# A latent attention and routed FFN layer: the 128-wide plain float32 products made into three products of high and low parts

## The chip, the cores and the metric

The kernel runs on one core of one Trainium2 chip. The metric is the device time of one execution in microseconds, the median of three runs.

## What is computed

A post-norm layer on `x[2, 512, 256]`: attention whose keys and values are one shared latent per position, then an FFN on the half of the positions that a router picks.

```python
k = x @ W_lat + b_lat                                  # [2, 512, 128], keys and values of all heads
q = (x @ W_d + b_d).reshape(Bx, Tx, NH, L)             # 16 heads of 128
att = jnp.einsum('bhtl,bsl->bhts', q, k) * scale
att = softmax(where(causal, att, -inf))
y = jnp.einsum('bhts,bsl->bhtl', att, k)
x = layernorm(x + (y @ W_proj + b_proj))
scores = jnp.einsum('bsd,d->bs', x, router_weight) + router_bias[0]
top_scores, indices = top_k(scores, 256)
processed = gelu(x[indices] @ w1 + b1) @ w2 + b2
x = layernorm(x.at[indices].add(processed * sigmoid(top_scores)))
```

## The kernel before

A unit is one head of one batch entry; there are 32. The 512 positions are four tiles of 128. Each engine has its own program of periods, and period p works on several units at once: scores of unit p, turning and values of unit p - 1, output projection of unit p - 2, queries of unit p + 1. The engines meet at semaphores alone, and each keeps its program order.

Nearly every product is done in three parts. Both operands are kept as a high part (rounded to float32r) and a low part (the remainder), and `product` (lines 359 to 364) issues high x high (L362), high x low (L363) and low x high (L364) into one PSUM bank. In the trace each of these is one weight load and one matmul. Two products are plain float32 instead, each one call in the code and two weight loads with two matmuls in the trace:

- line 441, in `scores`: the scores of the first query tile (j = 0), 128 queries against 128 keys, from `qT_first` and `kT`;
- line 511, in `values`: the last key tile's part of the values (i = 3), from `k_last` and `pT_last`, into the last 128 columns of `ps_y`.

Their operands are made on ScalarE (ACT): line 685 writes `qT_first` from the queries' PSUM bank, and line 687 the high part of the other 384 columns; VectorE (DVE) then writes their low part at line 836. For the probabilities, which TensorE (PE) turns by transposes (line 461, three groups in `turn`, listed in `turns` at line 225), the third group holds i = 3 and i = 2: line 723 copies i = 3 as `pT_last`, line 724 takes the high part of i = 2 and line 889 (DVE) its low part. For the keys themselves, once for each batch entry, line 703 writes `k_last`, line 704 and line 858 the parts of the other three tiles.

PE's order within a period, in the middle of the loop, is: scores of j = 3 and 2; turns 0 and 1; scores of j = 1 and 0; queries of the next unit (six matmuls of 512 columns); turn 2; projection (twelve matmuls of 256 columns); values i = 0 to 3. The matmuls that need `qT_lo` are the first scores of the next period; those that need the third turn's parts are the values of i = 2 and 3. After period 17 DVE adds the projection of the first batch entry to `x1` (`take_out`, line 1005, half by half), and the first projection of the second entry waits for it in period 18.

Of the kernel before, what the change touches and what calls it, by code (L numbers as in the profile page):

```python
# [28 lines left out]
F32 = mybir.dt.float32  # L29
F32R = mybir.dt.float32r  # L30
BF16 = mybir.dt.bfloat16
ACT = mybir.ActivationFunctionType
ALU = mybir.AluOpType

P = 128
BATCH, SEQ, DIM = 2, 512, 256
HEADS, LAT = 16, 128
FFN = 1024
KEEP = SEQ // 2
TILES = SEQ // P  # L40
# [9 lines left out]
P_OFF = [P * (j * (j + 1) // 2) for j in range(TILES)]  # L50
P_COLS = P * TILES * (TILES + 1) // 2

PT_OFF = {2: 0, 1: 2 * P, 0: 5 * P}
PT_COLS = 9 * P


def mk_layer_kernel(nc, x, W_lat, b_lat, W_d, b_d, W_proj, b_proj, router_w, router_b,
                    w1, b1, w2, b2, out):
    with ExitStack() as top:
        def sb(name, shape, dt=F32, stack=top):  # L60
            return stack.enter_context(nc.sbuf_tensor(name, shape, dt))

        def sem(name):
            return top.enter_context(nc.semaphore(name))
# [19 lines left out]
        bias_cols = sb("bias_cols", [P, BIASES])  # L84
# [37 lines left out]
        ps_s3, ps_s2, ps_s10, ps_t0, ps_t1, ps_y = bank  # L122
        ps_q = ps_s3
# [3 lines left out]
        def sems(name):  # L127
# [10 lines left out]
        x_turned, x_hi_done, x_split, x1_started = sem("x_turned"), sem("x_hi_done"), sem("x_split"), sem("x1_started")  # L138
        kT_ready, kT_done, kT_hi_done, kT_split = (
            sem(n) for n in ("kT_ready", "kT_done", "kT_hi_done", "kT_split"))  # L140
        k_turned, k_last_done, k_hi_done, k_split = (
            sem(n) for n in ("k_turned", "k_last_done", "k_hi_done", "k_split"))
        wd_hi_done, wd_split = sem("wd_hi_done"), sem("wd_split")
        wp_hi_done, wp_split = sem("wp_hi_done"), sem("wp_split")
        wf_hi_done, wf_split = sem("wf_hi_done"), sem("wf_split")
        q_ready, q_first_done, q_hi_done, q_lo_done = (
            sem(n) for n in ("q_ready", "q_first_done", "q_hi_done", "q_lo_done"))
        mask_done = sem("mask_done")
        scores_ready, negmax_done, exp_done, rinv_done = (
            sem(n) for n in ("scores_ready", "negmax_done", "exp_done", "rinv_done"))  # L150
        norm_act, norm_dve = sem("norm_act"), sem("norm_dve")
        pt_ready, pt_last_done, pt_hi_done, pt_lo_done = (
            sem(n) for n in ("pt_ready", "pt_last_done", "pt_hi_done", "pt_lo_done"))
        y_ready, y_hi_done, y_lo_done = sem("y_ready"), sem("y_hi_done"), sem("y_lo_done")
        proj_done, proj_half, out_taken = sem("proj_done"), sem("proj_half"), sem("out_taken")
        stats_done, aggr_done, var_done, rstd_done, ln_done = (
# [17 lines left out]
        def wait(eng, s, value):  # L174

            if not isinstance(value, int) or value > 0:
                eng.wait_ge(s, value)


        att = ExitStack()  # L180
# [5 lines left out]
        kT = [sb(f"kT{b}", [P, SEQ], F32, att) for b in range(BATCH)]  # L186
        kT_hi = [sb(f"kT_hi{b}", [P, SEQ], F32R, att) for b in range(BATCH)]
        kT_lo = [sb(f"kT_lo{b}", [P, SEQ], F32R, att) for b in range(BATCH)]
        k_hi = [sb(f"k_hi{b}", [P, TILES - 1, LAT], F32R, att) for b in range(BATCH)]
        k_lo = [sb(f"k_lo{b}", [P, TILES - 1, LAT], F32R, att) for b in range(BATCH)]  # L190
        k_last = [sb(f"k_last{b}", [P, LAT], F32, att) for b in range(BATCH)]

        wd_raw = [sb(f"wd_raw{s}", [P, CH, LAT], F32, att) for s in range(2)]
        wd_hi = [sb(f"wd_hi{s}", [P, CH, LAT], F32R, att) for s in range(2)]
# [2 lines left out]
        wp_hi = [sb(f"wp_hi{s}", [P, DIM], F32R, att) for s in range(2)]  # L197
        wp_lo = [sb(f"wp_lo{s}", [P, DIM], F32R, att) for s in range(2)]

        qT_first = [sb(f"qT_first{s}", [P, P], F32, att) for s in range(2)]  # L200
        qT_hi = [sb(f"qT_hi{s}", [P, SEQ], F32R, att) for s in range(2)]
        qT_lo = [sb(f"qT_lo{s}", [P, SEQ], F32R, att) for s in range(2)]
        yT_hi, yT_lo = sb("yT_hi", [P, SEQ], F32R, att), sb("yT_lo", [P, SEQ], F32R, att)
        probs = [sb(f"probs{s}", [P, P_COLS], F32, att) for s in range(2)]
        pT_last = sb("pT_last", [P, P], F32, att)
        pT_hi, pT_lo = sb("pT_hi", [P, PT_COLS], F32R, att), sb("pT_lo", [P, PT_COLS], F32R, att)
        att.close()

# [9 lines left out]
        def p_tile(s, j):  # L218
# [5 lines left out]

        turns = [([0], ps_t0, ps_t0[:, :], slice(PT_OFF[0], PT_OFF[0] + 4 * P)),
                 ([1], ps_t1, ps_t1[:, 0:3 * P], slice(PT_OFF[1], PT_OFF[1] + 3 * P)),
                 ([3, 2], ps_t0, ps_t0[:, P:3 * P], slice(PT_OFF[2], PT_OFF[2] + 2 * P))]

        class Period:

# [71 lines left out]
        ps_k = ps_out[:, 2:4, :].rearrange("p a d -> p (a d)")  # L302
# [55 lines left out]
        def _(pe):  # L358
            def product(dst, left, right, first=True, last=True, check=False):

                (lh, ll), (rh, rl) = left, right
                pe.matmul(dst, lh, rh, start=first, stop=False, skip_group_check=check)  # L362
                pe.matmul(dst, lh, rl, start=False, stop=False, skip_group_check=check)  # L363
                return pe.matmul(dst, ll, rh, start=False, stop=last, skip_group_check=check)  # L364
# [51 lines left out]
            for c in range(CH):  # L416
                last = product(ps_q[:, :], (wd_hi[0][:, c, :], wd_lo[0][:, c, :]),
                               (xT_hi[0][:, c, :], xT_lo[0][:, c, :]), c == 0, c == CH - 1)
# [5 lines left out]
            def scores(at, js):  # L424
                p, b, s = at.p, at.batch(0), at.place(0)
                if at.fixed == b * HEADS:
                    pe.wait_ge(kT_split, b + 1)
                    pe.wait_ge(kT_done, b + 1)
                for j in js:
                    n = (j + 1) * P  # L430
                    dst = score_bank[j]
                    if j == 3:
                        wait(pe, q_lo_done, p + 1)
                    if j:
                        wait(pe, negmax_done, p * 4 - {3: 3, 2: 2, 1: 0}[j])
                    t = slice(j * P, (j + 1) * P)
                    if j:
                        last = product(dst, (qT_hi[s][:, t], qT_lo[s][:, t]), (kT_hi[b][:, 0:n], kT_lo[b][:, 0:n]))
                    else:
                        wait(pe, q_first_done, p + 1)  # L440
                        last = pe.matmul(dst, qT_first[s][:, :], kT[b][:, 0:P], start=True, stop=True)  # L441
                    if j != 1:
                        last.then_inc(scores_ready, 1)

# [52 lines left out]
            def values(at):  # L497

                p, b = at.p, at.batch(-1)
                if at.fixed - 1 == b * HEADS:  # L500
                    pe.wait_ge(k_split, b + 1)
                    pe.wait_ge(k_last_done, b + 1)
                wait(pe, y_lo_done, p - 1)
                for i in range(TILES - 1):
                    wait(pe, pt_lo_done, p * 3 - 2 + i)
                    n = (TILES - i) * P
                    t = slice(PT_OFF[i], PT_OFF[i] + n)
                    product(ps_y[:, SEQ - n:], (k_hi[b][:, i, :], k_lo[b][:, i, :]),
                            (pT_hi[:, t], pT_lo[:, t]), i == 0, False)
                wait(pe, pt_last_done, p)  # L510
                pe.matmul(ps_y[:, SEQ - P:], k_last[b][:, :], pT_last[:, :], start=False, stop=True).then_inc(y_ready, 1)  # L511


            def turn_scores(b, dst):
# [164 lines left out]
        def _(act):  # L679
            def split_queries(k, place, head):  # L680

                wait(act, q_ready, k + 1)
                wait(act, scores_ready, k * 3 - 3)
                bias = bias_cols[:, bass.ds(head, 1)]
                act.activation(qT_first[place][:, :], ps_q[:, 0:P], ACT.Identity, bias=bias,
                               scale=1.0).then_inc(q_first_done, 1)
                act.activation(qT_hi[place][:, P:], ps_q[:, P:], ACT.Identity, bias=bias,  # L687
                               scale=1.0).then_inc(q_hi_done, 1)

            def x_high(b):  # L690
# [9 lines left out]

            def k_high(b):
                act.wait_ge(k_turned, b + 1)
                act.copy(k_last[b][:, :], ps_k[:, SEQ - P:]).then_inc(k_last_done, 1)
                act.copy(k_hi[b][:, :, :], ps_k[:, 0:SEQ - P].rearrange("p (j l) -> p j l", l=LAT)).then_inc(k_hi_done, 1)

            x_high(0)
            act.wait_ge(bias_done, 1)
# [11 lines left out]

            def turned(at, n):  # L720
                wait(act, pt_ready, at.p * 3 - 2 + n)
                if n == 2:
                    act.copy(pT_last[:, :], ps_t0[:, 0:P]).then_inc(pt_last_done, 1)
                act.copy(pT_hi[:, turns[n][3]], turns[n][2]).then_inc(pt_hi_done, 1)  # L724

            def period(at):
# [100 lines left out]
            for j in range(TILES):  # L827
                act.wait_ge(minus_mean_done, j // 2 + 1)
                act.activation(squared[:, j, :], x1[:, TILES + j, :], ACT.Square, bias=minus_mean[:, j:j + 1],  # L829
                               scale=1.0, accum_out=squares[:, j:j + 1]).then_inc(squares_done, 1)  # L830

        @block.vector
        def _(dve):
            def queries_low(k, place, head):
                wait(dve, q_hi_done, k + 1)
                dve.scalar_tensor_tensor(qT_lo[place][:, P:], ps_q[:, P:], bias_cols[:, bass.ds(head, 1)],  # L836
                                         qT_hi[place][:, P:].bitcast(F32), ALU.add, ALU.subtract).then_inc(q_lo_done, 1)

            dve.memset(still[:, :], 0.0).then_inc(still_filled, 1)

# [14 lines left out]

            def k_low(b):
                dve.wait_ge(k_hi_done, b + 1)
                dve.tensor_tensor(k_lo[b][:, :, :], ps_k[:, 0:SEQ - P].rearrange("p (j l) -> p j l", l=LAT),
                                  k_hi[b][:, :, :].bitcast(F32), ALU.subtract).then_inc(k_split, 1)

            dve.wait_ge(wlat_in, 16)
# [308 lines left out]
            for half in range(2):  # L1170
                for j in range(2 * half, 2 * half + 2):
                    add_up(1, j)
                t = slice(2 * half, 2 * half + 2)
# [3 lines left out]
            for half in range(2):  # L1177
                t = slice(2 * half, 2 * half + 2)
# [146 lines left out]
```

## Time and profile before

| | us |
|---|---|
| median of 3 runs | 300.29 (300.2 to 300.47) |
| the profiled execution | 299.99 |
| its span, first to last instruction | 298.3 |
| PE busy (matmuls) | 287.2 (96% of the span) |
| PEld busy (weight loads, beside PE) | 261.6 (88%) |
| DVE busy | 223.0 (75%) |
| ACT busy | 211.8 (71%) |
| POOL busy | 143.3 (48%) |

The granted clock of PE is full in 39 of the 40 slices of the page. A matmul's record is longer than the time by which it holds up the next one, since matmuls are pipelined, so their cost is read from start to start. The same holds, to a lesser degree, for ACT and DVE, whose records overlap a little.

### The profile page before, as it was taken

To read this page: it belongs to the slowest core of one execution; us is meant where nothing else is said; L and a number is where in the kernel's file an instruction comes from. 1 tells how busy PE (TensorE), PEld (TensorE's weight loads), DVE (VectorE), ACT (ScalarE), POOL (GpSimd) and SP (SyncE) were. 2 spreads that over 40 slices of the span, in tenths; PEclk is the share of its full clock that TensorE was granted. 3 is DMA by queue.
4 is the path that set the end of the run, shared out by engine and by line. 5 is a ranking of instruction groups with operands and counts; after the bars stand their busy time and mean duration, and the time that the engine had idled before them with its cause. 6 is when DMAs were issued, how large, how long until landed. Compare 5 with 4: busy or idle time off the path is not lost.

```text
span 298.3 us, 6300 instructions
## 1 busy us (share of the span) xinstructions
PE 287.2 (96%) x1942; PEld 261.6 (88%) x1942; DVE 223.0 (75%) x698; ACT 211.8 (71%) x582; POOL 143.3 (48%) x201
## 2 busy tenths in 40 slices
PE   7999999999999999999989999999999999999990
PEld 4787999999999999999889999999999999999990
DVE  3688777777777777777878788989778877497674
ACT  3588777777777777777767777777788777663622
POOL 3557533333333358555554755556556512183011
PEclk9999999999999999999999999999999999999998
DMA  6582111111111111111110111111110000000012
GB/s 196 105 302 72 52 37 35 35 35 35 34 33 30 39 41 34 35 32 36 32 36 18 34 37 35 38 35 35 38 36 20 19 21 0 2 1 0 2 45 96
DMA packets 17738, 13.42 MB, mean 45 GB/s; under 512 B 1433, under 2 KB 17458, under 8 KB 17714
## 3 DMA queue, kind: packets, MB, share of 16 engines
q1 hardware_dynamic: 17714, 13.13, 15.0%
q8 instruction: 12, 0.20, 0.2%
q14 instruction: 12, 0.10, 0.1%
HBM read 12.07 MB, written 1.05 MB: 44 GB/s over the span
## 4 chain that ended last, share of the span: by engine, by line
PE 87%; DVE 6%; ACT 2%; issue 1%; SPq 1%; DMA 1%; POOLq 0%; DVEq 0%; ACTq 0%
PE bank L362 17%; PE bank L364 16%; PE bank L363 16%; PE bank L461 11%; PE ps_out L362 6%; PE ps_out L364 6%; PE ps_out L363 6%; PE bank L511 2%; PE bank L441 2%; DVE x L1043 1%; DMA bias_rows<-in_L_ffn_b 1%; DVE x L1005 1%; ACT squared L829 1%; DVE sel L1051 1%; PE bank L550 1%
## 5 line engine op out<-in xcount | busy, mean ns | idle before, releaser
L717 ACT ACTIVATE probs<-probs,negmax 128x512 f32<-128x512 f32 (+3 forms) x128 | 72.6, 574 | 6.9 <-DVE negmax L882 5.5
L1197 POOL TENSOR_TENSOR wd_hi<-wd_raw,zero 128x256 fp32r<-128x256 f32 x32 | 24.6, 769 | 95.7 <-DVE probs L937 89.6
L724 ACT CAST pT_hi<-bank 128x512 fp32r<-128x512 f32 (+2 forms) x96 | 43.5, 488 | 33.1 <-PE bank L461 33.1
L889 DVE TENSOR_TENSOR pT_lo<-bank,pT_hi 128x512 fp32r<-128x512 f32 (+2 forms) x96 | 53.0, 553 | 11.1 <-ACT pT_hi L724 11.1
L882 DVE CUSTOM_DVE_ANT_0 probs<-bank,mask_row 128x512 f32<-128x512 f32 (+3 forms) x128 | 59.1, 482 | 0.6 <-PE bank L364 0.6
L461 PE MATMUL bank<-ident,probs 128*128 128x128 f32 x320 | 45.3, 272 | 0.0
L461 PEld LDWEIGHTS bank<-ident,probs 128*128 128x128 f32 x320 | 38.5, 140 | 5.3 <-issue 0.2
L362 PE MATMUL ps_out<-wp_hi,yT_hi 128*128 128x256 f32 x128 | 38.5, 301 | 1.1 <-DVE x L1005 1.1
L362 PE MATMUL bank<-kT_hi,qT_hi 128*128 128x512 f32 (+2 forms) x96 | 37.7, 393 | 0.2 <-DVE qT_lo L836 0.2
L899 DVE TENSOR_TENSOR yT_lo<-bank,yT_hi 128x512 fp32r<-128x512 f32 x32 | 22.1, 691 | 21.0 <-PE bank L364 14.8
L364 PE MATMUL ps_out<-wp_hi,yT_lo 128*128 128x256 f32 x128 | 36.2, 283 | 0.0
L363 PE MATMUL ps_out<-wp_lo,yT_hi 128*128 128x256 f32 x128 | 36.1, 282 | 0.0
L362 PE MATMUL bank<-pT_hi,k_hi 128*128 128x512 f32 (+2 forms) x96 | 32.9, 343 | 0.6 <-DVE pT_lo L889 0.6
L364 PE MATMUL bank<-kT_hi,qT_lo 128*128 128x512 f32 (+2 forms) x96 | 32.7, 340 | 0.0
L363 PE MATMUL bank<-pT_lo,k_hi 128*128 128x512 f32 (+2 forms) x96 | 32.4, 337 | 0.0
L363 PE MATMUL bank<-kT_lo,qT_hi 128*128 128x512 f32 (+2 forms) x96 | 32.3, 337 | 0.0
L364 PE MATMUL bank<-pT_hi,k_lo 128*128 128x512 f32 (+2 forms) x96 | 32.2, 335 | 0.0
L1197 POOL TENSOR_TENSOR wp_hi<-wp_raw,zero 128x256 fp32r<-128x256 f32 x32 | 23.6, 737 | 14.2 <-DVE probs L937 14.2
L756 ACT ACTIVATE probs<-probs,rinv 128x512 f32<-128x512 f32 x32 | 23.2, 726 | 8.2 <-DVE rinv L931 8.2
L937 DVE TENSOR_SCALAR probs<-probs,rinv 128x384 f32<-128x384 f32 (+2 forms) x96 | 28.1, 350 | 1.1
L836 DVE SCALAR_TENSOR_TENSOR qT_lo<-bank,bias_cols,qT_hi 128x384 fp32r<-128x384 f32 x32 | 19.8, 617 | 11.9 <-ACT qT_hi L687 11.4
L362 PE MATMUL bank<-xT_hi,wd_hi 128*128 128x512 f32 x64 | 27.9, 435 | 0.0
(148 smaller groups left out, 742.0 us busy)
## 6 DMA issues: line engine op xcount, KB each, us to landing
wd_raw<-in_L_attn_W_d SPq DMA_DIRECT2D x32, 128.0 KB, 2.2
wp_raw<-in_L_attn_W_proj SPq DMA_DIRECT2D x32, 128.0 KB, 2.1
wf_raw<-in_L_ffn_w SPq DMA_DIRECT2D x2, 1024.0 KB, 7.1
x_nat<-in_L_attn_x SPq DMA_DIRECT2D x4, 256.0 KB, 2.9
out<-x SPq DMA_DIRECT2D x3, 256.0 KB, 2.2
out<-x SPq DMA_DIRECT2D x2, 128.0 KB, 1.9
wlat_raw<-in_L_attn_W_lat SPq DMA_DIRECT2D x1, 128.0 KB, 3.3
bproj_all<-in_L_attn_b_proj SPq DMA_DIRECT2D x1, 128.0 KB, 3.5
```

Source lines behind the costliest of these rows:

```text
L362: pe.matmul(dst, lh, rh, start=first, stop=False, skip_group_check=check)
L363: pe.matmul(dst, lh, rl, start=False, stop=False, skip_group_check=check)
L364: return pe.matmul(dst, ll, rh, start=False, stop=last, skip_group_check=check)
L461: last = pe.transpose(dst[:, a:a + P], p_tile(s, j)[:, i * P:(i + 1) * P], ident[:, :])
L717: act.activation(p_tile(s, j), p_tile(s, j), ACT.Exp, bias=negmax[:, s, j:j + 1], scale=-1.0, accum_out=sums[:, s, j:j + 1]).then_inc(exp_ ...
L724: act.copy(pT_hi[:, turns[n][3]], turns[n][2]).then_inc(pt_hi_done, 1)
L756: act.mul(p_tile(at.place(0), 3), p_tile(at.place(0), 3), rinv[:, at.place(0), 3:4]).then_inc(norm_act, 1)
L882: dve.tensor_tensor_reduce(p_tile(s, j), score_bank[j], mask_row[:, (TILES - 1 - j) * P:], -SCALE, -MASKED, ALU.add, ALU.min, accum_out=ne ...
L889: dve.tensor_tensor(pT_lo[:, dst], src, pT_hi[:, dst].bitcast(F32), ALU.subtract).then_inc(pt_lo_done, 1)
L899: dve.tensor_tensor(yT_lo[:, :], ps_y[:, :], yT_hi[:, :].bitcast(F32), ALU.subtract).then_inc(y_lo_done, 1)
L937: dve.tensor_scalar(p_tile(s, j), p_tile(s, j), rinv[:, s, j:j + 1], None, ALU.mult).then_inc(norm_dve, 1)
L1197: pool.tensor_tensor(hi, src, nothing, ALU.add).then_inc(hi_done, 1)
```

## The change

The two plain products become calls of `product`. With them `qT_first`, `k_last` and `pT_last`, their semaphores and the ACT instructions that wrote them go; the instructions that write the high and low parts of queries, keys and of the third turn grow by 128 columns. The number of matmuls of these two products goes from 2 to 3 each, and all six become float32r matmuls with 128 moving columns.

```diff
-PT_OFF = {2: 0, 1: 2 * P, 0: 5 * P}
-PT_COLS = 9 * P
+PT_OFF = {3: 0, 2: P, 1: 3 * P, 0: 6 * P}
+PT_COLS = 10 * P
...
-                 ([3, 2], ps_t0, ps_t0[:, P:3 * P], slice(PT_OFF[2], PT_OFF[2] + 2 * P))]
+                 ([3, 2], ps_t0, ps_t0[:, 0:3 * P], slice(PT_OFF[3], PT_OFF[3] + 3 * P))]
...
-                    if j:
-                        last = product(dst, (qT_hi[s][:, t], qT_lo[s][:, t]), (kT_hi[b][:, 0:n], kT_lo[b][:, 0:n]))
-                    else:
-                        wait(pe, q_first_done, p + 1)
-                        last = pe.matmul(dst, qT_first[s][:, :], kT[b][:, 0:P], start=True, stop=True)
+                    last = product(dst, (qT_hi[s][:, t], qT_lo[s][:, t]), (kT_hi[b][:, 0:n], kT_lo[b][:, 0:n]))
...
-                for i in range(TILES - 1):
-                    wait(pe, pt_lo_done, p * 3 - 2 + i)
+                for i in range(TILES):
+                    if i < TILES - 1:
+                        wait(pe, pt_lo_done, p * 3 - 2 + i)
                     n = (TILES - i) * P
                     t = slice(PT_OFF[i], PT_OFF[i] + n)
-                    product(ps_y[:, SEQ - n:], (k_hi[b][:, i, :], k_lo[b][:, i, :]),
-                            (pT_hi[:, t], pT_lo[:, t]), i == 0, False)
-                wait(pe, pt_last_done, p)
-                pe.matmul(ps_y[:, SEQ - P:], k_last[b][:, :], pT_last[:, :], start=False, stop=True).then_inc(y_ready, 1)
+                    last = product(ps_y[:, SEQ - n:], (k_hi[b][:, i, :], k_lo[b][:, i, :]),
+                                   (pT_hi[:, t], pT_lo[:, t]), i == 0, i == TILES - 1)
+                last.then_inc(y_ready, 1)
...
-                act.activation(qT_first[place][:, :], ps_q[:, 0:P], ACT.Identity, bias=bias,
-                               scale=1.0).then_inc(q_first_done, 1)
-                act.activation(qT_hi[place][:, P:], ps_q[:, P:], ACT.Identity, bias=bias,
+                act.activation(qT_hi[place][:, :], ps_q[:, :], ACT.Identity, bias=bias,
                                scale=1.0).then_inc(q_hi_done, 1)
...
-                act.copy(k_last[b][:, :], ps_k[:, SEQ - P:]).then_inc(k_last_done, 1)
-                act.copy(k_hi[b][:, :, :], ps_k[:, 0:SEQ - P].rearrange("p (j l) -> p j l", l=LAT)).then_inc(k_hi_done, 1)
+                act.copy(k_hi[b][:, :, :], ps_k.rearrange("p (j l) -> p j l", l=LAT)).then_inc(k_hi_done, 1)
...
-                if n == 2:
-                    act.copy(pT_last[:, :], ps_t0[:, 0:P]).then_inc(pt_last_done, 1)
                 act.copy(pT_hi[:, turns[n][3]], turns[n][2]).then_inc(pt_hi_done, 1)
...
-                dve.scalar_tensor_tensor(qT_lo[place][:, P:], ps_q[:, P:], bias_cols[:, bass.ds(head, 1)],
-                                         qT_hi[place][:, P:].bitcast(F32), ALU.add, ALU.subtract).then_inc(q_lo_done, 1)
+                dve.scalar_tensor_tensor(qT_lo[place][:, :], ps_q[:, :], bias_cols[:, bass.ds(head, 1)],
+                                         qT_hi[place][:, :].bitcast(F32), ALU.add, ALU.subtract).then_inc(q_lo_done, 1)
...
-                dve.tensor_tensor(k_lo[b][:, :, :], ps_k[:, 0:SEQ - P].rearrange("p (j l) -> p j l", l=LAT),
+                dve.tensor_tensor(k_lo[b][:, :, :], ps_k.rearrange("p (j l) -> p j l", l=LAT),
                                   k_hi[b][:, :, :].bitcast(F32), ALU.subtract).then_inc(k_split, 1)
```

## Rows read from the trace of the kernel before

**Rows 1.** The page: part 1 (busy us) and part 4 (chain that ended last)

```profile
PE 287.2 (96%) x1942; PEld 261.6 (88%) x1942; DVE 223.0 (75%) x698; ACT 211.8 (71%) x582; POOL 143.3 (48%) x201
...
PE 87%; DVE 6%; ACT 2%; issue 1%; SPq 1%; DMA 1%; POOLq 0%; DVEq 0%; ACTq 0%
```

**Rows 2.** Waits of PE: us in total, times, longest us

```profile
PE ps_out L362 <- DVE x L1005: 1.1, 1, 1.1
PE bank L362 <- DVE pT_lo L889: 0.6, 1, 0.6
```

**Rows 3.** Timeline, PE, one period: start us, us, engine, line, out<-in

```profile
121.70 0.28 PE L364 MATMUL bank<-pT_hi,k_lo 128*128 128x256 f32 x1
121.81 0.39 PE L511 MATMUL bank<-pT_last,k_last 128*128 128x128 f32 x2
121.95 0.47 PE L362 MATMUL bank<-kT_hi,qT_hi 128*128 128x512 f32 x1
122.27 0.39 PE L363 MATMUL bank<-kT_lo,qT_hi 128*128 128x512 f32 x1
122.50 0.40 PE L364 MATMUL bank<-kT_hi,qT_lo 128*128 128x512 f32 x1
...
124.39 0.38 PE L441 MATMUL bank<-kT,qT_first 128*128 128x128 f32 x2
...
124.84 0.40 PE L363 MATMUL bank<-xT_lo,wd_hi 128*128 128x512 f32 x1
...
128.99 0.28 PE L362 MATMUL bank<-pT_hi,k_hi 128*128 128x256 f32 x1
```

**Rows 4.** Timeline, PEld (weight loads), the same period, around L441

```profile
124.27 0.31 PEld L441 LDWEIGHTS bank<-kT,qT_first 128*128 128x128 f32 x2
124.50 0.19 PEld L362 LDWEIGHTS bank<-xT_hi,wd_hi 128*128 128x128 f32 x1
124.61 0.19 PEld L363 LDWEIGHTS bank<-xT_lo,wd_hi 128*128 128x128 f32 x1
```

**Rows 5.** Timeline, PEld, the first two loads after a stall

```profile
23.48 0.19 PEld L362 LDWEIGHTS bank<-pT_hi,k_hi 128*128 128x128 f32 x1 [0.97 <-DVE pT_lo L889]
23.59 0.19 PEld L363 LDWEIGHTS bank<-pT_lo,k_hi 128*128 128x128 f32 x1
```

**Rows 6.** Bf16 loads: timeline of ten matmuls, then line 525 (ns min/median/max)

```profile
214.07 0.39 PE L525 MATMUL bank<-ones_bf,beats 128*128 128x1 bf16 x10
...
L525 PEld LDWEIGHTS bank<-ones_bf,beats x20: 95/96/100, 214.0 to 271.8; 128*128 128x128 bf16 x20
```

**Rows 7.** Groups by shape, ACT: busy us, mean ns, idle before

```profile
L687 ACT ACTIVATE qT_hi<-bank,bias_cols 128x384 fp32r<-128x384 f32 x32 | 18.2, 570 | 0.0
...
L724 ACT CAST pT_hi<-bank 128x384 fp32r<-128x384 f32 x32 | 15.6, 486 | 0.0
...
L724 ACT CAST pT_hi<-bank 128x256 fp32r<-128x256 f32 x32 | 12.5, 390 | 0.0
L685 ACT ACTIVATE qT_first<-bank,bias_cols 128x128 f32<-128x128 f32 x32 | 11.3, 354 | 1.0 <-PE bank L364 1.0
L723 ACT COPY pT_last<-bank 128x128 f32<-128x128 f32 x32 | 8.4, 262 | 0.0
...
L698 ACT ACTIVATE kT_hi<-ps_out,bias_cols 128x512 fp32r<-128x512 f32 x2 | 1.4, 678 | 2.1 <-PE ps_out L364 2.1
```

**Rows 8.** Groups by shape, DVE

```profile
L836 DVE SCALAR_TENSOR_TENSOR qT_lo<-bank,bias_cols,qT_hi 128x384 fp32r<-128x384 f32 x32 | 19.8, 617 | 11.9 <-ACT qT_hi L687 11.4
L889 DVE TENSOR_TENSOR pT_lo<-bank,pT_hi 128x384 fp32r<-128x384 f32 x32 | 17.7, 552 | 0.0
...
L889 DVE TENSOR_TENSOR pT_lo<-bank,pT_hi 128x256 fp32r<-128x256 f32 x32 | 13.3, 415 | 0.3 <-ACT pT_hi L724 0.3
...
L853 DVE SCALAR_TENSOR_TENSOR kT_lo<-ps_out,bias_cols,kT_hi 128x512 fp32r<-128x512 f32 x2 | 1.5, 737 | 2.0 <-ACT kT_hi L698 2.0
```

**Rows 9.** Timeline, DVE, the third turn's low part in the same period

```profile
127.84 0.41 DVE L889 TENSOR_TENSOR pT_lo<-bank,pT_hi 128x256 fp32r<-128x256 f32 x1
```

More of the change, by code:

```diff
@@ L140, in mk_layer_kernel @@
             sem(n) for n in ("kT_ready", "kT_done", "kT_hi_done", "kT_split"))
-        k_turned, k_last_done, k_hi_done, k_split = (
-            sem(n) for n in ("k_turned", "k_last_done", "k_hi_done", "k_split"))
+        k_turned, k_hi_done, k_split = (sem(n) for n in ("k_turned", "k_hi_done", "k_split"))
         wd_hi_done, wd_split = sem("wd_hi_done"), sem("wd_split")
@@ L145, in mk_layer_kernel @@
         wf_hi_done, wf_split = sem("wf_hi_done"), sem("wf_split")
-        q_ready, q_first_done, q_hi_done, q_lo_done = (
-            sem(n) for n in ("q_ready", "q_first_done", "q_hi_done", "q_lo_done"))
+        q_ready, q_hi_done, q_lo_done = (sem(n) for n in ("q_ready", "q_hi_done", "q_lo_done"))
         mask_done = sem("mask_done")
@@ L151, in mk_layer_kernel @@
         norm_act, norm_dve = sem("norm_act"), sem("norm_dve")
-        pt_ready, pt_last_done, pt_hi_done, pt_lo_done = (
-            sem(n) for n in ("pt_ready", "pt_last_done", "pt_hi_done", "pt_lo_done"))
+        pt_ready, pt_hi_done, pt_lo_done = (sem(n) for n in ("pt_ready", "pt_hi_done", "pt_lo_done"))
         y_ready, y_hi_done, y_lo_done = sem("y_ready"), sem("y_hi_done"), sem("y_lo_done")
@@ L188, in mk_layer_kernel @@
         kT_lo = [sb(f"kT_lo{b}", [P, SEQ], F32R, att) for b in range(BATCH)]
-        k_hi = [sb(f"k_hi{b}", [P, TILES - 1, LAT], F32R, att) for b in range(BATCH)]
-        k_lo = [sb(f"k_lo{b}", [P, TILES - 1, LAT], F32R, att) for b in range(BATCH)]
-        k_last = [sb(f"k_last{b}", [P, LAT], F32, att) for b in range(BATCH)]
+        k_hi = [sb(f"k_hi{b}", [P, TILES, LAT], F32R, att) for b in range(BATCH)]
+        k_lo = [sb(f"k_lo{b}", [P, TILES, LAT], F32R, att) for b in range(BATCH)]
         wd_raw = [sb(f"wd_raw{s}", [P, CH, LAT], F32, att) for s in range(2)]
@@ L198, in mk_layer_kernel @@
         wp_lo = [sb(f"wp_lo{s}", [P, DIM], F32R, att) for s in range(2)]
-        qT_first = [sb(f"qT_first{s}", [P, P], F32, att) for s in range(2)]
         qT_hi = [sb(f"qT_hi{s}", [P, SEQ], F32R, att) for s in range(2)]
@@ L204, in mk_layer_kernel @@
         probs = [sb(f"probs{s}", [P, P_COLS], F32, att) for s in range(2)]
-        pT_last = sb("pT_last", [P, P], F32, att)
         pT_hi, pT_lo = sb("pT_hi", [P, PT_COLS], F32R, att), sb("pT_lo", [P, PT_COLS], F32R, att)
@@ L427, in scores @@
                     pe.wait_ge(kT_split, b + 1)
-                    pe.wait_ge(kT_done, b + 1)
                 for j in js:
@@ L501, in values @@
                     pe.wait_ge(k_split, b + 1)
-                    pe.wait_ge(k_last_done, b + 1)
                 wait(pe, y_lo_done, p - 1)
-                for i in range(TILES - 1):
-                    wait(pe, pt_lo_done, p * 3 - 2 + i)
+                for i in range(TILES):
+                    if i < TILES - 1:
+                        wait(pe, pt_lo_done, p * 3 - 2 + i)
                     n = (TILES - i) * P
                     t = slice(PT_OFF[i], PT_OFF[i] + n)
-                    product(ps_y[:, SEQ - n:], (k_hi[b][:, i, :], k_lo[b][:, i, :]),
-                            (pT_hi[:, t], pT_lo[:, t]), i == 0, False)
-                wait(pe, pt_last_done, p)
-                pe.matmul(ps_y[:, SEQ - P:], k_last[b][:, :], pT_last[:, :], start=False, stop=True).then_inc(y_ready, 1)
+                    last = product(ps_y[:, SEQ - n:], (k_hi[b][:, i, :], k_lo[b][:, i, :]),
+                                   (pT_hi[:, t], pT_lo[:, t]), i == 0, i == TILES - 1)
+                last.then_inc(y_ready, 1)
             def turn_scores(b, dst):
```

## The prediction

> **What bounds the kernel now.** I read the page first, then PE's waits, then one period of the attention loop in the timeline. PE is busy for 96% of the span and holds 87% of the chain that ended last [rows 1]. In the attention part it stands still only twice for longer than half a microsecond: 1.1 us for `take_out` on DVE (L1005), and 0.6 us in the second period for the low part of the third turn (L889) [rows 2]. In the middle of the loop one matmul follows the other for the whole period of 7.5 us. So what the change adds to PE's own sequence in a period is added to the time, and what it saves or costs on ACT and DVE counts only where it makes PE wait.
>
> **What sets a 128-wide matmul.** The record of a matmul (0.27 to 0.48 us) is its latency, so I read starts. A float32r matmul of 512 columns holds up the next for 0.23 us (122.27 to 122.50), one of 256 columns for 0.11 to 0.12 us (121.70 to 121.81) [rows 3]: both are 0.45 ns a column with next to nothing fixed, which would make 0.06 us for 128 columns. But every matmul here has its own weight load, and a load starts when the matmul before it has really begun, so there is at most one load under one matmul. How long a load takes is seen after a stall, where no matmul stands in its way: the loads of L362 and L363 start at 23.48 and 23.59, 0.11 us apart [rows 5]. The same 0.11 us is between the loads at 124.50 and 124.61 [rows 4], in the middle of the loop. At 256 columns the load is just hidden (0.11 under 0.12 us); at 128 columns it is not (0.11 against 0.06 us). I take 0.11 us for each float32r matmul of 128 columns; the trace has none, so this is read across from the loads. The two bounds of it below are the columns alone (0.06 us) and the rate of a plain product (0.22 us, next paragraph).
>
> **The change part by part.**
>
> PE, removed: two plain products in each of 32 units, 64 in all. One has two loads and two matmuls [rows 3, 4]. L441 starts at 124.39 and the matmul that follows it really begins when the load after its own starts, at 124.61, so the pair costs 0.22 us. The other place agrees: L511 starts at 121.81, the second 512-wide matmul behind it at 122.27, and with 0.23 us for the first of these the pair has cost 0.23 us [rows 3].
>
> PE, added: three float32r matmuls of 128 columns in each place, 3 x 0.11 = 0.33 us. The load of the first is hidden under the 256-wide matmul ahead of it, as now; but the load of the 512-wide matmul behind sits under the third, as it now sits under the second, and so three loads' time passes either way. The difference is 0.33 - 0.22 = 0.11 us a product, 64 x 0.11 = 7.0 us, all on the path. With 0.10 and 0.12 us, for the reading of starts to 0.01 us, it is 6.4 to 7.7 us.
>
> ACT, queries: L685 and L687 have 354 and 570 ns; one instruction of 512 columns of the same form has 678 ns (L698) [rows 7]. The sum of records falls by 0.25 us, but records overlap; by half of that at the least I take 0.12 us. DVE's low part of the queries grows from 617 ns to about 737 ns, what L853 takes for 512 columns in the same form [rows 8]. So `qT_lo` is ready between 0.13 us earlier and about when it is now, and PE uses it only after queries, projection and values. Nothing.
>
> ACT and DVE, third turn: L723 and L724 (262 + 390 ns) become one copy of 384 columns, 486 ns [rows 7]; DVE's L889 goes from 415 to 552 ns [rows 8]. The result comes between 0.03 us earlier and 0.14 us later. It is done at 127.84 + 0.41 = 128.25 us [rows 9], and the values of i = 2, which need it, begin at 128.99 [rows 3]: a cover of 0.74 us. Without the cover it would cost at most 0.14 us a period, 4.5 us in all. The values of i = 3 now wait for nothing of their own. Where nothing lies between, in the second period, the wait of 0.6 us [rows 2] ends up to 0.1 us later, but PE also comes to it 0.11 us later by its first longer product; I take zero there. The last unit's values have no queries ahead of them, and I allow 0.1 us.
>
> Keys: L703 and L704 become one instruction, L858 grows by 128 columns, twice in the program and before the loop is in step: between -0.1 and +0.1 us each, and I take zero.
>
> Waits: those for `qT_first`, `k_last` and `pT_last` go, none had a stall to its name, and none is added. DVE gets some 0.26 us more in a period that grows by 0.22 us; it is busy for 75% of the span [rows 1], so it does not become the bound.
>
> Given back: in period 18 PE waits 1.1 us for L1005 [rows 2]. The longer scores of j = 0 bring PE there 0.11 us later, while DVE comes to L1005 through the turns and the maxima, which it gets before. The wait shrinks by 0.1 us.
>
> Sum: 299.99 (the profiled execution: span 298.3 and 1.7 us around it) + 7.0 + 0.1 - 0.1 = 307.0 us. That execution is 0.3 us below the median of 300.29 us, so in the median 300.29 + 7.0 = 307.3 us. I put it at 307.2, since the wait at L1005 is the surer of the two small terms.
>
> The Trainium skill, page "TensorE: Matmul & The Clock Gate", section "Back-to-back issue gap", gives about 81 ns for a load and its matmul in a steady stream at 128 columns. By that, as an estimate from the page, three would cost 0.24 us, and the change 1.5 us in all: 301.8 us. The loads in this trace say 0.11 us, and I go by them.
>
> **The rivals.**
>
> Narrow float32r runs at the plain rate. If a float32r matmul of 128 columns had no gain over plain float32, each of the three would cost what the plain product costs, 0.22 us: 0.66 instead of 0.22 us, 64 x 0.44 = 28 us, so 328.5 us. For it: no row has a float32r matmul below 256 columns. Against it: from 512 to 256 columns the cost goes down in proportion, with no sign of a step [rows 3].
>
> The load does not bind, and the change is faster. If the load of a short matmul could run under more than one matmul, or were short, the three would cost their columns, 3 x 0.06 = 0.18 us against 0.22 us: -0.04 x 64 = -2.6 us, 297.7 us. It decides as soon as a load and matmul together take less than 0.073 us, a third of the plain product. For it: ten bf16 loads and matmuls of L525 take 0.39 us together, under 0.04 us each, and their load records are 96 ns [rows 6], so there are short loads on this engine. Against it: the float32r loads have records of 0.19 us like those of the plain ones, and are 0.11 us apart where nothing holds them [rows 4, 5]. The Trainium skill, same page, section "Weight-path perf modes — Fast Weight Load (FWL) and DoubleRow", says that the fast load is on for 128 weights of any type that isn't FP32. If float32r counted as another type, this rival would be the forecast; by the rows its loads are as long as those of FP32.
>
> That the stall moves elsewhere (DVE late for the third turn) is no rival of size: it would add at most the 4.5 us above to the forecast, and it has 0.74 us of cover.
>
> **How the numbers follow.** Forecast 0.85, with a range of its own of 306.4 to 308.3 us: 300.29 + 6.4 - 0.1 for the wait and - 0.2 for the keys, and 300.29 + 7.7 + 0.1 + 0.2. Narrow at the plain rate 0.08. Load not binding 0.07, of which 0.05 faster than before and 0.02 in between (steps of more than 0.073 but less than 0.10 us, so slower). The range is the forecast's own, widened by 0.5 us each way for what adds up unseen in the start, the tail and the run to run difference: 305.9 to 308.8 us. The rivals lie far outside it, and 0.85 less a small tail is the 8 in 10 wanted. A change of under 0.2% (0.6 us), about what a measurement of this kernel can tell from no change, has 0.01; faster 0.05, slower 0.94.
>
> **What would show it.** In the profile after: L441 and L511 gone, three 128-wide float32r matmuls in each place, 64 more matmuls under each of L362 to L364; their starts 0.11 us apart and the loads with them; a period longer by 0.22 us; PE's wait for L1005 at 1.0 us; ACT's busy time down by about 13 us, 32 x (0.25 + 0.17), and DVE's up by 8 us, 32 x (0.12 + 0.14). Starts 0.06 us apart would prove the load free, 0.22 us the plain rate. A new wait of PE for `pT_lo` or `qT_lo` in every period would prove the cover of ACT and DVE wrong.

## The result and the profile after

| | us |
|---|---|
| before, median | 300.28 (300.2 to 300.47) |
| after, median | 306.88 (306.55 to 306.96) |
| ratio | 1.0214 (95% interval 1.0191 to 1.0236) |
| after, the profiled execution | 306.90, span 305.2 |

The change makes the kernel 6.6 us slower; the spans of the two profiled executions differ by 6.9 us. On the page of the kernel after, busy time by engine and the chain that ended last answer to [rows 1]:

```profile
span 305.2 us, 6358 instructions
...
PE 293.3 (96%) x2006; PEld 268.4 (88%) x2006; DVE 230.0 (75%) x698; ACT 206.2 (68%) x516; POOL 143.5 (47%) x201
...
PE 87%; DVE 6%; ACT 2%; issue 1%; SPq 1%; DMA 1%; POOLq 0%; DVEq 0%; ACTq 0%
```

PE still holds 87% of the chain. It has 64 more matmuls and 6.1 us more busy time.

The timeline of PE around the scores of the first query tile, in the middle of the loop, answers to [rows 3] (`product` is now at lines 356 to 358):

```profile
127.50 0.28 PE L358 MATMUL bank<-kT_hi,qT_lo 128*128 128x256 f32 x1
127.62 0.22 PE L356 MATMUL bank<-kT_hi,qT_hi 128*128 128x128 f32 x1
127.68 0.28 PE L357 MATMUL bank<-kT_lo,qT_hi 128*128 128x128 f32 x1
127.79 0.27 PE L358 MATMUL bank<-kT_hi,qT_lo 128*128 128x128 f32 x1
127.90 0.44 PE L356 MATMUL bank<-xT_hi,wd_hi 128*128 128x512 f32 x1
128.18 0.39 PE L357 MATMUL bank<-xT_lo,wd_hi 128*128 128x512 f32 x1
```

and its weight loads (PEld) in the same stretch answer to [rows 4]:

```profile
127.62 0.19 PEld L357 LDWEIGHTS bank<-kT_lo,qT_hi 128*128 128x128 f32 x1
127.73 0.19 PEld L358 LDWEIGHTS bank<-kT_hi,qT_lo 128*128 128x128 f32 x1
127.84 0.19 PEld L356 LDWEIGHTS bank<-xT_hi,wd_hi 128*128 128x128 f32 x1
127.95 0.19 PEld L357 LDWEIGHTS bank<-xT_lo,wd_hi 128*128 128x128 f32 x1
```

Each of the three narrow matmuls stands between loads that start 0.11 us apart: 127.62, 127.73, 127.84 and 127.95. The load at 127.95 is under the first 512-wide matmul, which begins only then, although its record starts at 127.90. From the beginning of the first narrow matmul (127.62, where the load after its own starts) to that of the wide one it is 0.33 us; the plain pair had taken 0.22 us [rows 3, 4].

The two matmuls of the queries' first product in every unit mark the attention loop. In the line of `wd_hi` (count, ns min/median/max, first and last start in us), after and then before:

```profile
L356 PE MATMUL bank<-xT_hi,wd_hi x64: 389/397/465, 8.5 to 247.1; 128*128 128x512 f32 x64
```

```profile
L362 PE MATMUL bank<-xT_hi,wd_hi x64: 389/398/481, 8.2 to 240.7; 128*128 128x512 f32 x64
```

From the first to the last start it was 232.5 us and is 238.6 us, so 6.1 of the 6.9 us lie there, with 60 of the 64 products. Behind it are 0.5 us, with the other four. The 0.3 us ahead of it (8.2 to 8.5) are not of the change, since none of its products stands there: PE waited 1.3 us instead of 0.4 us for the DMA of `bias_rows` in this execution. A period in the middle of the loop took 7.53 us before (124.84 [rows 3] to 132.37; 7.51 and 7.53 in turn) and takes 7.74 us after (120.44 to 128.18 above), which is the 0.22 us forecast:

```profile
132.37 0.39 PE L363 MATMUL bank<-xT_lo,wd_hi 128*128 128x512 f32 x1
```

```profile
120.44 0.39 PE L357 MATMUL bank<-xT_lo,wd_hi 128*128 128x512 f32 x1
```

Of PE's waits, those of [rows 2] now read:

```profile
PE ps_out L356 <- DVE x L988: 1.0, 1, 1.0
PE bank L356 <- DVE pT_lo L872: 0.6, 1, 0.6
```

### The profile page after: what moved, and what is told of

Same layout as the page of the kernel before. It is cut to its first block, busy times and chain, and to the rows that moved or that the text cites. A ratio compares the mean times of both kernels' runs of the same rounds, so it can differ in the third digit from the quotient of the medians.

```text
span 305.2 us, 6358 instructions
## 1 busy us (share of the span) xinstructions
PE 293.3 (96%) x2006; PEld 268.4 (88%) x2006; DVE 230.0 (75%) x698; ACT 206.2 (68%) x516; POOL 143.5 (47%) x201
## 4 chain that ended last, share of the span: by engine, by line
PE 87%; DVE 6%; ACT 2%; issue 1%; SPq 1%; DMA 1%; POOLq 0%; DVEq 0%; ACTq 0%
PE bank L356 18%; PE bank L357 18%; PE bank L358 18%; PE bank L450 11%; PE ps_out L356 6%; PE ps_out L358 6%; PE ps_out L357 6%; DMA bias_rows<-in_L_ffn_b 1%; DVE x L1026 1%; DVE x L988 1%; ACT squared L812 1%; DVE sel L1034 1%; PE bank L536 1%; PE bank L538 1%; DVE beats L1061 1%
## 5 line engine op out<-in xcount | busy, mean ns | idle before, releaser
L707 ACT CAST pT_hi<-bank 128x384 fp32r<-128x384 f32 (+1 forms) x96 | 46.0, 514 | 35.4 <-PE bank L450 35.3
L872 DVE TENSOR_TENSOR pT_lo<-bank,pT_hi 128x384 fp32r<-128x384 f32 (+1 forms) x96 | 57.3, 597 | 11.9 <-ACT pT_hi L707 11.9
L356 PE MATMUL bank<-kT_hi,qT_hi 128*128 128x512 f32 (+3 forms) x128 | 44.0, 344 | 0.3 <-DVE qT_lo L819 0.2
L357 PE MATMUL bank<-kT_lo,qT_hi 128*128 128x512 f32 (+3 forms) x128 | 41.4, 323 | 0.0
L357 PE MATMUL bank<-pT_lo,k_hi 128*128 128x512 f32 (+3 forms) x128 | 41.3, 323 | 0.0
L358 PE MATMUL bank<-kT_hi,qT_lo 128*128 128x512 f32 (+3 forms) x128 | 41.1, 321 | 0.0
L358 PE MATMUL bank<-pT_hi,k_lo 128*128 128x512 f32 (+3 forms) x128 | 40.9, 319 | 0.0
L356 PE MATMUL bank<-pT_hi,k_hi 128*128 128x512 f32 (+3 forms) x128 | 40.0, 313 | 0.6 <-DVE pT_lo L872 0.6
L714 ACT CAST yT_hi<-bank 128x512 fp32r<-128x512 f32 x32 | 18.8, 586 | 18.3 <-PE bank L358 18.1
L819 DVE SCALAR_TENSOR_TENSOR qT_lo<-bank,bias_cols,qT_hi 128x512 fp32r<-128x512 f32 x32 | 24.0, 750 | 9.3 <-ACT qT_hi L673 9.1
```

The costliest lines, as they stand in the source:

```text
L819: dve.scalar_tensor_tensor(qT_lo[place][:, :], ps_q[:, :], bias_cols[:, bass.ds(head, 1)], qT_hi[place][:, :].bitcast(F32), ALU.add, ALU.s ...
L872: dve.tensor_tensor(pT_lo[:, dst], src, pT_hi[:, dst].bitcast(F32), ALU.subtract).then_inc(pt_lo_done, 1)
```

## The experiments

All variants are timed beside the kernel before on their own chip, whose median was 300.16 to 300.22 us there. The theory is that of the prediction: a matmul holds up the next for the longer of its own columns' time and the next weight load, a load of 128 float32 columns takes 0.11 us, and only the count of such loads decided the result.

**Each place alone.** First the scores only (a copy of the kernel before with this edit, and ACT and DVE writing all 512 columns of the queries; `...` in the cuts of code stands for what is left out):

```diff
-                    if j:
-                        last = product(dst, ...)
-                    else:
-                        last = pe.matmul(dst, qT_first[s][:, :], kT[b][:, 0:P], start=True, stop=True)
+                    last = product(dst, (qT_hi[s][:, t], qT_lo[s][:, t]), (kT_hi[b][:, 0:n], kT_lo[b][:, 0:n]))
```

> The kernel before with only the first query tile's scores made into three products; values, keys and the third turn as before. Load theory (each 128-wide float32r matmul costs its weight load of 0.11 us, one load more per product, nothing on ACT or DVE counts): half the change, 32 x 0.11 = 3.5 us less 0.1 us given back in the wait for L1005, 300.3 + 3.4 = 303.7 us. Rival, that one of the two places carries the cost (by a wait on ACT or DVE that the change moved): this kernel stands at either end, 300.3 or 306.9 us.

Measured: 304.22 us in the median of four, but as two pairs, 303.1 and 303.2, 305.2 and 305.2 us. The profile fell on one of the longer ones. Its PE timeline ahead of the loop:

```profile
6.47 0.29 PE L410 MATMUL bank<-ident,bias_rows 25*128 25x25 f32 x1 [0.74 <-DMA bias_rows<-in_L_ffn_b]
...
8.38 0.63 PE L361 MATMUL ps_out<-xT_lo,wlat_hi 128*128 128x512 f32 x1
8.80 0.63 PE L362 MATMUL ps_out<-xT_hi,wlat_lo 128*128 128x512 f32 x1
9.23 0.63 PE L360 MATMUL ps_out<-xT_hi,wlat_hi 128*128 128x512 f32 x1
9.66 0.63 PE L361 MATMUL ps_out<-xT_lo,wlat_hi 128*128 128x512 f32 x1
```

Matmuls of 512 columns start 0.42 to 0.43 us apart up to 10.1 us, 512 / 0.43 = 1190 columns in a microsecond, as at the lower of the two clock levels (1.2 GHz), although the granted clock of the stretch is recorded as full. The same kernel once more:

> The scores-only kernel once more, since two of its four executions were 2.0 us longer than the other two with the whole difference ahead of the loop. Load theory: 303.2 us with a period of 7.62 to 7.63 us, as in the shorter two. If the long start belongs to this kernel, 305.2 us comes again.

Measured: 303.13 us (302.99 to 303.43, ten executions), 3.0 us above the median of the kernel before beside it (300.17 us). The measured ratio is lower, 1.0084 (1.0062 to 1.0105), since three of the thirteen executions of the kernel before took 302.0 us. In the profile of this kernel the same matmuls are 0.22 to 0.23 us apart:

```profile
5.64 0.30 PE L410 MATMUL bank<-ident,bias_rows 25*128 25x25 f32 x1
...
7.36 0.39 PE L361 MATMUL ps_out<-xT_lo,wlat_hi 128*128 128x512 f32 x1
7.58 0.39 PE L362 MATMUL ps_out<-xT_hi,wlat_lo 128*128 128x512 f32 x1
7.81 0.40 PE L360 MATMUL ps_out<-xT_hi,wlat_hi 128*128 128x512 f32 x1
```

The first start of `wd_hi` is at 10.44 us in the long execution and at 8.51 us here. Of these 1.9 us, 0.8 lie ahead of L410, which waited for the DMA of `bias_rows` in the long one, and 1.1 in the slower pace. The long start comes and goes with an execution and is no part of the edit: the kernel before also has executions some 2 us longer (five, beside the variants on two chips), though none of these was profiled. Then the values only (the kernel after with the scores put back):

```diff
-                    last = product(dst, (qT_hi[s][:, t], qT_lo[s][:, t]), (kT_hi[b][:, 0:n], kT_lo[b][:, 0:n]))
+                    if j:
+                        last = product(dst, ...)
+                    else:
+                        wait(pe, q_first_done, p + 1)
+                        last = pe.matmul(dst, qT_first[s][:, :], kT[b][:, 0:P], start=True, stop=True)
```

> The changed kernel with the first query tile's scores put back to one plain float32 product; the last key tile's values stay three products. Load theory: 32 x 0.11 = 3.5 us, 303.7 to 303.8 us, and with the scores-only kernel the two gains sum to the whole of 6.6 to 7.0 us. Rival, that one place carries the cost: the opposite end from the scores-only kernel.

Measured: 303.26 us (303.19 to 303.36), ratio 1.0104 (1.0087 to 1.012). The two places cost 3.0 and 3.1 us, together 6.1 of the 6.6 us. Neither carries the cost alone; they are 0.5 and 0.4 us under the 3.5 us of the theory. Their steady periods are 7.62 to 7.63 us, 0.10 us and a little more above the 7.52 us before, where both together add 0.22 us; why the two halves fall short of the whole is open.

**The count of matmuls.** Two terms instead of three in the narrow products:

```diff
                 pe.matmul(dst, lh, rh, start=first, stop=False, skip_group_check=check)
+                if dst.shape[1] == P:
+                    return pe.matmul(dst, lh, rl, start=False, stop=last, skip_group_check=check)
                 pe.matmul(dst, lh, rl, start=False, stop=False, skip_group_check=check)
```

(`dst` is 128 columns wide in these two places alone; `lh, rh` and `rl` are the high and low parts of the two operands.)

> The changed kernel with two of the three matmuls in the two 128-wide products (low x high is left out there, so part of the sum is missing). ACT and DVE work is that of the changed kernel. Load theory: two loads as in the plain product, so the time of before, 300.3 us (299.9 to 300.6), and the steady period 7.52 us. Rival, that the ACT and DVE side of the change costs or gains something on the path: the distance from 300.3 us is that amount. Rival, that a matmul of the first 128-wide float32r product is cheap and the later ones dear (an uneven step): 64 x (another amount than 0.11 us) less than 306.9 us.

Measured: 299.98 us (ten executions), ratio 0.9993 (0.9983 to 1.0002). With ACT and DVE as in the kernel after and as many loads as before, the whole 6.6 us are gone. What the change does on ACT and DVE neither costs nor gains anything on the path that shows within some 0.5 us. And four terms:

```diff
                 pe.matmul(dst, lh, rh, start=first, stop=False, skip_group_check=check)
+                if dst.shape[1] == P:
+                    pe.matmul(dst, ll, rl, start=False, stop=False, skip_group_check=check)
```

> The changed kernel with a fourth matmul, low x low, in the two 128-wide products. Load theory: one more load each, 64 x 0.11 = 7.0 us, 306.9 + 7.0 = 313.9 us, period 7.96 us. Rival, that the cost of the change sits in the switch between kinds of matmul or in ACT and DVE and not in the count of loads: less, down to 64 x 0.06 = 3.8 us for the columns alone, 310.7 us.

Measured: 313.59 us (313.52 to 313.8), ratio 1.0447 (1.043 to 1.0465). The weight loads around the scores of the first tile:

```profile
122.83 0.19 PEld L358 LDWEIGHTS bank<-kT_lo,qT_lo 128*128 128x128 f32 x1
122.94 0.19 PEld L359 LDWEIGHTS bank<-kT_lo,qT_hi 128*128 128x128 f32 x1
123.06 0.19 PEld L360 LDWEIGHTS bank<-kT_hi,qT_lo 128*128 128x128 f32 x1
123.17 0.19 PEld L356 LDWEIGHTS bank<-xT_hi,wd_hi 128*128 128x128 f32 x1
123.28 0.19 PEld L359 LDWEIGHTS bank<-xT_lo,wd_hi 128*128 128x128 f32 x1
```

Again 0.11 to 0.12 us from one to the next, now four times. Two, three and four matmuls give 299.98, 306.88 and 313.59 us: 6.9 and 6.7 us for each further matmul in 64 places, 0.108 and 0.105 us. The lines of `wd_hi` for two and for four:

```profile
L356 PE MATMUL bank<-xT_hi,wd_hi x64: 387/398/467, 8.4 to 240.6; 128*128 128x512 f32 x64
```

```profile
L356 PE MATMUL bank<-xT_hi,wd_hi x64: 389/398/450, 8.7 to 253.5; 128*128 128x512 f32 x64
```

From first to last start 232.2 and 244.8 us, with 238.6 us for three between them. The steady periods are 7.52, 7.74 and 7.95 us.

**Load or columns.** The count alone can't say whether a narrow matmul takes 0.11 us for its load or for its 128 columns at half their rate. First half the moving columns, for the second and third matmul of each narrow product:

```diff
+                if dst.shape[1] == P:
+                    pe.matmul(dst, lh, rh, start=first, stop=last)
+                    pe.matmul(dst[:, 0:64], lh, rl[:, 0:64], start=False, stop=False, skip_group_check=True)
+                    return pe.matmul(dst[:, 0:64], ll, rh[:, 0:64], start=False, stop=last, skip_group_check=True)
```

> The changed kernel with the second and third matmul of the two 128-wide products on 64 moving columns instead of 128 (the low parts' terms are missing for the other 64 columns); their weights keep 128 columns. Load theory: the load of 0.11 us binds whatever the columns, no change, 306.9 us. Rival, that a narrow float32r matmul streams its columns at about half rate (128 in 0.11 us): 64 x 2 x 0.055 = 7.0 us less, 299.9 us.

Measured: 306.25 us (306.0 to 306.54), ratio 1.0196 (1.016 to 1.0232). 0.6 us less than the kernel after where the columns' theory wanted 7.0 us. The loads have not moved together:

```profile
127.01 0.19 PEld L358 LDWEIGHTS bank<-kT_lo,qT_hi 128*128 128x128 f32 x1
127.12 0.19 PEld L359 LDWEIGHTS bank<-kT_hi,qT_lo 128*128 128x128 f32 x1
127.23 0.19 PEld L360 LDWEIGHTS bank<-xT_hi,wd_hi 128*128 128x128 f32 x1
127.34 0.19 PEld L361 LDWEIGHTS bank<-xT_lo,wd_hi 128*128 128x128 f32 x1
```

Then half the stationary columns of the same two matmuls, with 128 moving columns:

```diff
+                    pe.matmul(dst[0:64, :], lh[:, 0:64], rl, start=False, stop=False, skip_group_check=True)
+                    return pe.matmul(dst[0:64, :], ll[:, 0:64], rh, start=False, stop=last, skip_group_check=True)
```

> The changed kernel with the second and third matmul of the two 128-wide products on 64 of the 128 stationary columns (so the low parts' terms are missing for half of the output partitions); moving columns stay 128. Load theory, if a load's time goes with its stationary columns: 0.055 us a load, so two steps of the product fall from 0.11 to the 0.06 us of the columns, 64 x 2 x 0.05 = 6.4 us less, 300.5 us. If a load's time is fixed whatever its columns: 306.9 us. Rival, half rate columns: 306.9 us too, but then the kernel with 64 moving columns is the fast one.

Measured: 300.57 us (ten executions, 300.18 to 302.63), ratio 1.0007 (0.9985 to 1.003).

```profile
124.49 0.19 PEld L357 LDWEIGHTS bank<-kT_hi,qT_hi 128*128 128x128 f32 x1
124.61 0.13 PEld L358 LDWEIGHTS bank<-kT_lo,qT_hi 128*64 128x64 f32 x1
124.67 0.14 PEld L359 LDWEIGHTS bank<-kT_hi,qT_lo 128*64 128x64 f32 x1
124.73 0.19 PEld L360 LDWEIGHTS bank<-xT_hi,wd_hi 128*128 128x128 f32 x1
124.84 0.19 PEld L361 LDWEIGHTS bank<-xT_lo,wd_hi 128*128 128x128 f32 x1
```

The loads of 64 columns start at 124.61 and 124.67 and the next at 124.73: 0.06 us each, with records of 0.13 and 0.14 us instead of 0.19. Half the moving columns gave 0.6 us and half the stationary columns gave 6.3 us back, as the load theory had it. The step of 0.06 us is also that of the 128 moving columns (0.45 ns each), so it bounds the load of 64 columns from above and does not measure it. Such a matmul also writes 64 output partitions instead of 128. No run separates that from the load; the shorter load records speak for the load. Third, twice the moving columns for the scores of the first tile:

```diff
-                    n = (j + 1) * P
-                    dst = score_bank[j]
+                    n = (j + 1) * P if j else 2 * P
+                    dst = score_bank[j] if j else ps_s10[:, 0:2 * P]
```

> The changed kernel with the first query tile's scores taken against 256 keys instead of 128 (the other 128 columns go into a part of the bank that nobody reads). Load theory: the three steps go from the load's 0.11 us to the columns' 0.117 us, 32 x 3 x 0.007 = 0.7 us, 307.6 us. Rival, half rate columns: 32 x 3 x 0.11 = 10.6 us more if the rate holds, 317 us; if the full rate comes back at 256 columns, 307.6 us as well.

Measured: 307.04 us (306.85 to 307.42), ratio 1.0221 (1.0184 to 1.0258). The further 128 columns are nearly free, 0.2 us in all, which is within the spread of the runs. That is less than the 0.7 us of the theory by its own small figures.

**One load ahead, or more.** The three narrow matmuls put between the 512-wide ones of the next unit's queries:

```diff
+                for m, (w, v) in enumerate(wide):
+                    last = pe.matmul(ps_q[:, :], w, v, start=m == 0, stop=m == 5, skip_group_check=True)
+                    if m < 3:
+                        first = pe.matmul(score_bank[0], *narrow[m], start=m == 0, stop=m == 2, skip_group_check=True)
+                        if m == 2:
+                            first.then_inc(scores_ready, 1)
```

> The changed kernel with the three 128-wide matmuls of the first query tile's scores put one by one between the 512-wide matmuls of the next unit's queries, instead of ahead of them. Load theory with one load ahead (a load starts when the matmul before it begins): each step is the longer of its columns and the next load, so the narrow one still costs 0.11 us; no gain, 306.9 us, perhaps 0.1 to 0.2 us less where a delayed load behind the narrow ones falls away. Rival, that loads can run more than one ahead so that the wide matmul's slack of 0.12 us hides the narrow one's load: 32 x 3 x 0.05 = 4.8 us less, 302.1 us. The scores are ready 0.7 us later for DVE, which has 1.5 us before it comes to them.

Measured: 309.22 us (309.06 to 309.36), ratio 1.0291 (1.0255 to 1.0327), 2.3 us slower than the kernel after, which neither side expected. The loads and then DVE's last instruction for the row maxima of j = 3 in the same period:

```profile
120.99 0.19 PEld L472 LDWEIGHTS bank<-xT_hi,wd_hi 128*128 128x128 f32 x1
121.10 0.19 PEld L474 LDWEIGHTS bank<-kT_hi,qT_hi 128*128 128x128 f32 x1
121.34 0.19 PEld L472 LDWEIGHTS bank<-xT_lo,wd_hi 128*128 128x128 f32 x1
121.44 0.19 PEld L474 LDWEIGHTS bank<-kT_lo,qT_hi 128*128 128x128 f32 x1
121.68 0.19 PEld L472 LDWEIGHTS bank<-xT_hi,wd_lo 128*128 128x128 f32 x1
121.79 0.19 PEld L474 LDWEIGHTS bank<-kT_hi,qT_lo 128*128 128x128 f32 x1
```

```profile
120.79 0.08 DVE L883 DVE_READ_ACCUMULATOR2_ANT negmax<- 128x1 f32 x1
```

The loads are in turn 0.24 and 0.10 to 0.11 us apart, wide and narrow: the wide one's slack does not shorten the narrow one, so on its own question this kernel says one load ahead. The rest is a wait that I had not costed. The queries use the bank of the scores of j = 3 and wait until DVE has read it (`negmax_done`). With the three narrow matmuls no longer ahead of them they come 0.33 us earlier, DVE's record ends at 120.87, and the first wide load starts at 120.99, 0.07 us after the matmul ahead of it began (120.92). Nor is it this period alone: in 30 of the 31 periods that have both, the first wide load starts 0.05 to 0.12 us after the end of DVE's record, and in 25 of the 31 it is 0.07 us or more behind the start of the matmul ahead; in the kernel after it starts 0.29 to 0.40 us behind DVE's record in the middle of the loop. From the first to the last start of `wd_hi`, where these periods lie, this kernel takes 1.9 us more than the kernel after, out of the 2.3 us. The times point to the bank; no run takes that wait away. The same question without a wait in play, the last key tile's three in turn with the three 256-wide matmuls of the tile before:

```diff
+                for m, (k, pT) in enumerate(((k_hi, pT_hi), (k_hi, pT_lo), (k_lo, pT_hi))):
+                    for i in (2, 3):
+                        ...
+                        last = pe.matmul(ps_y[:, SEQ - n:], k[b][:, i, :], pT[:, t], start=False,
+                                         stop=(m == 2 and i == 3))
```

> The changed kernel with the last key tile's three 128-wide matmuls taken in turn with the three 256-wide ones of the tile before (wide, narrow, wide, narrow, wide, narrow) instead of behind them; no wait is moved and none can become late by it. One load ahead: each step is the longer of its own columns and the next load, 3 x (0.12 + 0.11), no change, 306.9 us, period 7.74 us. Rival, that loads can run further ahead and so the wide ones' slack and the narrow ones' excess average out: 3 x (0.117 + 0.06), 32 x 3 x 0.05 = 4.8 us less, 302.1 us.

Measured: 306.38 us (306.24 to 306.44), ratio 1.0205 (1.0188 to 1.0222). 0.5 us less than the kernel after, a tenth of the 4.8 us that loads further ahead would give; the steady period is 7.73 us. Neither of the two orders tried hides the narrow ones' loads, and none of the kernels that compute the whole layer is faster than the kernel before.

## Why the prediction was right

Forecast 307.2 us, measured 306.88 us. Step by step:

- **PE's own sequence is the bound.** Held. Its waits of over half a microsecond in the attention part are the same two, and the kernel with two terms shows nothing else of the change on the path.
- **0.22 us for the plain pair, 0.33 us for the three.** Held: 0.33 us in the timeline after, and 0.22 us more in a steady period with two products. Read over all, one matmul more in 64 places is 6.7 to 6.9 us, 0.105 to 0.108 us each, at the low side of the bounds of 0.10 and 0.12. That the load and not the columns sets it was read across from the loads after a stall [rows 5]; the pair with 64 moving and with 64 stationary columns shows it.
- **The fixed rate of 0.22 us for narrow float32r, and the free load.** Both fell: they stood for 328.5 and 297.7 us. The step of 0.06 us of the second rival is real, but only with 64 stationary columns. The Trainium skill's 81 ns for load and matmul at 128 columns (page "TensorE: Matmul & The Clock Gate", section "Back-to-back issue gap") does not hold for float32r here: the trace has 0.11 us. The Trainium skill, same page, section "LDWEIGHTS (loading the stationary operand)", gives a load as its columns over 1.2 GHz; by an estimate from the page that is 107 ns for 128 columns and 53 ns for 64. The loads 0.11 us apart agree with it, and the 0.06 us for 64, as an upper bound, do not contradict it.
- **ACT and DVE under cover.** Held, by the same rows. L819 takes 750 ns for 512 columns (forecast 737), L872 550 ns for 384 (552), L673 677 ns (678), L707 477 ns (486):

```profile
L707 ACT CAST pT_hi<-bank 128x384 fp32r<-128x384 f32 x64 | 30.5, 477 | 0.1
...
L673 ACT ACTIVATE qT_hi<-bank,bias_cols 128x512 fp32r<-128x512 f32 x32 | 21.7, 677 | 1.5 <-PE bank L358 1.0
```

```profile
L872 DVE TENSOR_TENSOR pT_lo<-bank,pT_hi 128x384 fp32r<-128x384 f32 x64 | 35.2, 550 | 0.4 <-ACT pT_hi L707 0.4
L819 DVE SCALAR_TENSOR_TENSOR qT_lo<-bank,bias_cols,qT_hi 128x512 fp32r<-128x512 f32 x32 | 24.0, 750 | 9.3 <-ACT qT_hi L673 9.1
```

The low part of the third turn is done at 123.32 + 0.55 = 123.87 us, and PE takes it up at 124.58, so 0.71 us of the cover of 0.74 us are left:

```profile
123.32 0.55 DVE L872 TENSOR_TENSOR pT_lo<-bank,pT_hi 128x384 fp32r<-128x384 f32 x1
```

```profile
124.58 0.28 PE L356 MATMUL bank<-pT_hi,k_hi 128*128 128x256 f32 x1
```

- **DVE and ACT busy time.** DVE rose by 7.0 us (forecast 8). ACT fell by 5.6 us, not 13: I had added up records, and those of ACT overlap, so the page counts their union. The ACT groups of the queries and turns alone did fall by the forecast amount, from 66.0 us (18.2 + 11.3 + 15.6 + 12.5 + 8.4, [rows 7]) to 52.2 us (30.5 + 21.7, above). The warning that records overlap stood in the prediction, and the forecast of the busy time did not heed it. The time did not hang on it.
- **0.1 us given back at L1005.** Held: 1.1 to 1.0 us; with the fourth matmul it is 0.9 us.
- **The small excess.** 0.3 us of the forecast is too much. The steady periods have the full 0.22 us. Between the first queries and the fourth, PE has four of the products, 0.44 us by the forecast, and the three periods grow by only 0.23 us; the third of them, which holds the 0.6 us wait for the third turn, grows by 0.07 us where two products stand. The period with the wait at L1005 grows by 0.11 us, as forecast, and the three longer ones near the end by 0.18 to 0.19 us. So most of the excess lies in the periods at the start, where the prediction took zero for the wait, and not in the step; no run takes that wait away.

## What to carry to other kernels

Cost a narrow float32r matmul by its weight load: 0.11 us for 128 stationary columns, whatever it streams up to some 240 columns (an estimate, 0.11 us over 0.45 ns; 64, 128 and 256 columns were run). Three products of parts lose to one plain float32 product here, at 128 columns, where the plain product takes two loads and the three parts three. Whether they win where the columns are many is not shown: no row has a plain float32 matmul of more than 128 moving columns. Before splitting a small product or adding a term, count loads, and to lighten it cut stationary columns, not moving ones. Two of the three loads of `product` are of the same operand (high x high and high x low share the stationary high part), and the trace has a load for each; a form that loads it once was not tried.

## What the runs showed of the hardware

- A float32r load takes time by its stationary columns, 0.11 us for 128 and at most 0.06 us for 64. With 128 stationary columns the moving columns of a matmul, 64, 128 or 256 of them, change little: halved in 128 matmuls they took 0.6 us off the kernel, doubled in 96 they added 0.2 us.
- A load runs under one matmul only, for float32r with 128 stationary columns: with wide and narrow matmuls in turn the steps stay 0.24 and 0.10 to 0.11 us.
- One kernel started in two ways, 2.0 us apart. In the profile of each, PE's first float32r products of 512 columns took 0.43 or 0.23 us, which made 1.1 us, and the matmul of `bias_rows`, which waits for a DMA, came 0.8 us later in the long one, while the granted clock was recorded as full in both. Why is open.
